# Index columns of a gather copied one group ahead on GpSimd, in a graph network kernel

## The reference

```python
def _L0_gnn_ref(x, edge_index, W1, b1, g1, be1, W2, b2, g2, be2):
    src, dst = edge_index
    edge_features = jnp.concatenate([x[src], x[dst]], axis=1)
    h = edge_features @ W1.T + b1
    h = jax.nn.relu(_batchnorm(h, g1, be1))      # over all edges
    h = h @ W2.T + b2
    edge_updates = jax.nn.relu(_batchnorm(h, g2, be2))
    return jax.ops.segment_sum(edge_updates, dst, num_segments=x.shape[0])
```

## Time and profile before

| | us |
|---|---|
| Median of 3 runs | 4666.78 |
| Lowest and highest run | 4644.99, 4670.69 |
| Profiled execution, whole time | 4677.76 |
| Its span, first to last instruction | 4675.8 |

### The profile page before, as it was taken

The page is one execution under the profiler, slowest core; times in us unless marked ns, Lnnn a source line. Parts: engine busy times, 40 slices in busy tenths (PEclk is TensorE's granted clock), DMA queues, the critical chain, the costliest instruction groups (busy, mean ns, idle before and its releaser), DMA issues. The chain is left out here.

```text
span 4675.8 us, 83038 instructions
## 1 busy us (share of the span) xinstructions
PE 3483.7 (75%) x19041; PEld 1627.4 (35%) x19142; DVE 2879.6 (62%) x3796; ACT 1415.7 (30%) x1952; POOL 1093.9 (23%) x1131
## 2 busy tenths in 40 slices
PE   3776666574889888888877775377789947769994
PEld 2332222252444466665443333122222212222222
DVE  6887767537444455551021113499889949979993
ACT  1123334400222222221011111111088821118880
POOL 3777777666444122120000001000000000000000
PEclk8988878867999899997979997555599955559996
DMA  2345555645999633334838882722033362213331
GB/s 61 115 149 175 185 185 204 211 143 198 350 360 363 234 114 109 101 90 100 251 82 190 187 192 51 133 56 49 21 125 119 112 100 51 54 31 117 125 101 27
DMA packets 808847, 657.35 MB, mean 141 GB/s; under 512 B 599017, under 2 KB 686184, under 8 KB 808516
## 3 DMA queue, kind: packets, MB, share of 16 engines
q1 hardware_dynamic: 677642, 361.12, 29.1%
q10 hardware_dynamic: 106050, 243.93, 15.1%
q0 software_dynamic: 25088, 51.43, 4.3%
HBM read 316.58 MB, written 196.24 MB: 110 GB/s over the span
## 5 line engine op out<-in xcount | busy, mean ns | idle before, releaser
L637 POOL DMA_INDIRECT gat<-a_table,gidx x784 | 908.2, 1158 | 498.9 <-issue 272.7
L1371 DVE CUSTOM_DVE_ANT_0 masked<-psum,mask 128x1564 bf16<-128x1564 f32 x400 | 698.8, 1784 | 176.8 <-ACT mask L937 118.1
L1713 PE MATMUL psum<-qp,kp 96*128 96x391 bf16 x1600 | 589.5, 523 | 285.6 <-DVE mx L1371 160.5
L1406 DVE SCALAR_TENSOR_TENSOR pw<-ex,c_full 128x1564 f32<-128x1564 f32 x400 | 680.8, 1781 | 50.3 <-ACT ex L964 31.5
L1459 PE MATMUL psum<-one_src,one_dst 128*128 x1968 | 471.8, 381 | 271.5 <-issue 153.4
L964 ACT ACTIVATE ex<-psum 128x782 f32<-128x782 f32 x800 | 610.0, 826 | 77.8 <-PE psum L1735 59.8
L1125 DVE TENSOR_SCALAR one_src<-iota_sub,src_low 128x800 f16 x984 | 383.2, 430 | 200.2 <-issue 99.6
L1511 PE MATMUL psum<-c_ring,hp 128*128 128x512 bf16 (+1 forms) x2064 | 422.5, 360 | 75.2 <-DMA c_ring<-c_parts 53.1
L1713 PEld LDWEIGHTS psum<-qp,kp 96*128 x1600 | 173.5, 128 | 701.1 <-issue 701.1
L1459 PEld LDWEIGHTS psum<-one_src,one_dst 128*128 x1968 | 201.0, 106 | 525.9 <-issue 458.2
L1744 PE MATMUL psum<-pw,vaug 128*32 128x391 f32 x3200 | 348.8, 508 | 29.8 <-DVE pw L1406 9.4
(11 more groups left out here) (331 smaller groups left out, 3520.1 us busy)
## 6 DMA issues: line engine op xcount, KB each, us to landing
c_full<-c_whole SPq DMA_DIRECT2D x80, 977.5 KB, 5.0
a_edges<-gat SPq DMA_DIRECT2D x196, 256.0 KB
a_in<-a_edges ACTq DMA_DIRECT2D x98, 512.0 KB
r_edges<-r ACTq DMA_DIRECT2D x98, 512.0 KB
r_in<-r_edges SPq DMA_DIRECT2D x98, 512.0 KB, 3.5
c_whole<-c_sum ACTq DMA_DIRECT2D x100, 400.0 KB
dst_bc<-dst_half ACTq DMA_DIRECT2D x98, 256.0 KB
c_parts<-c_hi ACTq DMA_DIRECT2D x100, 200.0 KB
```

Of the source, the lines that this page charges most:

```text
L637: g.indirect_dma_start(gat[:, s, 2 * k * P:2 * (k + 1) * P], None, a_table, bass.IndirectOffsetOnAxis(ap=gidx[:, s, k:k + 1], axis=0)).the ...
L1371: v.tensor_tensor_reduce(out=masked[:, n % 2, :].rearrange("p (c t) -> p c t", c=4), in0=psum[:, o:o + 4 * BANK].rearrange("p (c t) -> p c ...
L1406: v.scalar_tensor_tensor(pw[:, step_slot(k), :].rearrange("p (h t) -> p h t", h=HQ), ex[:, step_slot(k), :].rearrange("p (h t) -> p h t", ...
L1713: last = t.matmul(bank((n % 2) * 4 + c, CW), kp[0:KQK, n // 2, ds(b * P, P)], qp[0:KQK, n // 2, ((n % 2) * 4 + c) * CW:((n % 2) * 4 + c + ...
```

## The change

There is a new helper `take_rows(i, s)` with the copy alone. In `gather`, the copy of the following group's columns, into the next place of `gidx`, is issued ahead of this group's waits and transfers; the wait on `row_sb` keeps its number, so it now asks for a copy issued one group before. The copy no longer stands behind `gat_free`. The first group's copy stands ahead of everything, and the last round of four stands behind the loop, since its last group has no follower. Number, size and order of the transfers and of the copies stay.

```diff
-            def gather(i):
+            def take_rows(i, s):
+                g.tensor_copy(gidx[:, s, :], src_i[:, ds(16 * i + 4 * s, 4)]).then_inc(S["row_sb"], 1)
+
+            def gather(i, more):
                 for s in range(4):
+                    if s < 3:
+                        take_rows(i, s + 1)
+                    elif more:
+                        take_rows(i + 1, 0)
                     after(pool, gat_free[s], i)
-                    g.tensor_copy(gidx[:, s, :], src_i[:, ds(16 * i + 4 * s, 4)]).then_inc(S["row_sb"], 1)
                     hold("pool", pool, S["row_sb"], 4 * i + s + 1)
...
-                        if k % 2 == 0 and (s or not isinstance(i, int)):
+                        if k % 2 == 0 and (s or not isinstance(i, int) or i):
...
-            gather(0)
-            with pool.Fori(1, NG // 4) as i:
-                gather(i)
+            take_rows(0, 0)
+            gather(0, True)
+            with pool.Fori(1, NG // 4 - 1) as i:
+                gather(i, True)
+            gather(NG // 4 - 1, False)
```

## The result

The changed kernel took 4600.15 us in the median of 5 runs (4595.63 to 4609.23), the kernel before beside it 4666.78 in 5 runs (4644.99 to 4671.9). The ratio is 0.986, 95% interval 0.983 to 0.989. The forecast was 4663, range 4641 to 4678: wrong, 63 us too high. And that is only half of the result. On two other chips, measured later, the same changed kernel is 14.5% and 14.7% **slower** than the kernel before. Both come from the two points that the prediction settled with one sentence each: what the gather does to the other engines, and whether it is off the path.

A forecast was written before the change was run, and what follows sets the result against it. The first pass was taken as held by DMA while the gather runs and by PE afterwards; -4.7 + 0.7 + 0.4 = -3.6 us took the profiled 4677.8 to 4674, 11 us above the median scale, so 4663 us, range 4641 to 4678.

The forecast's parts named there:

- The gather is off the path: First pass: the gather is never late, no stage waits for its end, and it touches the path by its bytes alone.
- Step 1: GpSimd, gap between copy and next transfer: 0.60 us a group saved of 0.88, bounds 0 and 0.86.
- Step 2: Stages ahead of the first pass: 80 us saved on GpSimd, so 12 groups move out of the first pass.
- Step 3: Gather in the first pass: pace stays 8.7 us a group, the gather ends 104 us sooner, near 1439 us.
- Step 4: First pass: 24 units run without the gather, 4.20 us each instead of 4.40, a gain of 4.7 us.
- Its cover: First pass: PE takes whatever DMA gives back beyond 0.20 us a unit.
- Step 5: Stages ahead of the first pass: the denser gather costs 0.7 us by bytes and 0.4 us by slower DVE one-hots.
- Bytes: Rival, first pass: with DMA full, 12 groups' bytes at 362 GB/s give 17 us, time 4651; chance 0.12.
- the gap stays: Rival, GpSimd: the gap stays 0.88 us or DVE's hold-up takes the saving; no group moves, 4667 us; chance 0.20.
- The counting stage pays: Rival, counting stage: denser gather makes ACT's window stores land late, PE waits longer; +45 us, 4712; chance 0.05.
- the second rival: GpSimd: the rival that the gap stays 0.88 us or DVE's hold-up takes all that is saved; chance 0.20.
- no difference: Whole kernel: the change can't be told from none, within about 0.5%, 23 us; chance 0.87, faster 0.07, slower 0.06.

The follow-up runs named there:

- before_again: The kernel before, unchanged, profiled once more on chip 13; 4622.72 us in one execution.
- deep3: The changed kernel with up to three pairs of gather transfers in flight instead of two, on chip 13; 4586.16 us, 0.986 of the kernel before.
- after_fourth: The changed kernel, unaltered, run again on chip 3; 5421.93 us, 1.147 of the kernel before.
- late: The changed kernel with the gather started only behind the counting stage, on chip 0; 5218.21 us.
- beforedeep: The kernel before with up to three pairs of gather transfers in flight instead of two, on chip 6; 4817.67 us, 1.023 of the kernel before.

## Why the prediction was wrong, point by point

**"The gather is off the path", the premise, failed.** It rests on the earlier trace rows, the last gather transfer 37 us ahead of the last load. That was true of that execution. It was not true of the kernel: the earlier trace rows holds because the counting stage was 76 us longer there than in `before_again`, where nothing stalled, and without them the last loads come one by one behind the gather, 13 us apart. The trace had the sign of it. The register rows of L1459 and L1125 are from that profile, and so is PE's wait for "issue", 107.0 us, the largest of its waits in 351 to 927 us. I read the earlier trace rows, which are about data, and never asked why two engines that wait for each other were both idle with nothing to wait for.

**Step 1** was right in kind. The gap fell from 0.88 to 0.16 us, 0.72 us a group, where I took 0.60 and the bounds were 0 and 0.86: an unwaited copy is followed after 0.16 us, another transfer after 0.30. **Step 2** was too small: in the pair without stalls 142 groups had been started when the first pass began, and 162 with the change, 20 more, where I took 12. A group of the counting stage took 6.16 us there instead of 7.09. The gap gives 0.72 of these 0.93 us; and the transfers, which I expected to be held up longer, were shorter, 1146 ns on average instead of 1229. In the profiled pair 160 groups were started (161 copies, 125 + 16 + 20, the last one ahead of its group) against 151, although there were 73 us less.

**Step 3** held for the pace: (1411 - 1091)/35 = 9.1 us a group in the first pass, 8.7 taken. That the gather ended only 28 us below the 1439 I gave is luck: the pass began 73 us earlier than in the forecast, and the gather ended 320 us into it, not 275. **Step 4** held for the execution that I argued from: with the gather 314.0/71 = 4.42 us a unit, behind it 97.0/24 = 4.04 (I said 4.40 and 4.20), and the pass was 6.4 us shorter for my 4.7. Its cover was the failed part: the pass had two limits, DMA and PE, and I left out the third, the gather's own end, since the premise had ruled it out. It is worth 39 us where the stage before is undisturbed.

**Step 5** priced what the denser gather costs the stages ahead at +1.1 us, by bytes and by 17 ns of one-hots a transfer. Without stalls it is near that: the counting stage ends at 851.4 and 854.5 us with the change, 850.6 before, 846.4 without any gather. In the profiled pair the stage went the other way, by -72.6 us, for the kernel before had stalls there and the changed one none; this is the larger part of what was measured, and no step of the prediction had it. Where the changed kernel stalls, the cost is +700 us or more: 1697 and 1723 us on chips 0 and 3, against 947 and 997 for the kernel before on chip 6 (of chips 0 and 3 there is no profile of it; its medians there are within 0.2% of chip 6's, and with three pairs in flight it ends counting at 958 on chip 0).

**The rivals.** "Bytes" and "the gap stays" are out by the unit times and the gap. The 362 GB/s that the bytes rival reckons with are no ceiling either: six stretches of 25 us of `deep3`, from 1100 to 1250 us, moved 364 to 382 GB/s. "The counting stage pays" named the right place, and for chips 0 and 3 the right sign, with a mechanism that plays no part (stores that land late; PE's waits for ACT's copies were 62.5 us in `after_fourth` and 77.8 in the changed kernel on the first chip) and, at 45 us of some 700, a fifteenth of the size. The hold-up of GpSimd by DVE that the second rival rested on fits the runs: in `after_fourth`, where DVE is busy for 271 of 1160 us beside the gather, a transfer takes 1001 ns on average, against 1172 in the counting stage of the changed kernel on the first chip (DVE busy for 637 of 774 us) and 1244 in that of the kernel before (642 of 846 us). That DVE is what holds it is read from these numbers; no run changes DVE's work alone. The cost of the gather for PE and DVE comes by their sequencers, whose register instructions took up to 1426 and 1415 ns there.

**The chances.** I gave 0.87 to "no difference" on one profile of one chip. The measured ratio, 0.983 to 0.989, is clear of 1. I took the spread of three runs, 26 us, for noise around one shape of the execution. The spread could have told that something differs between executions by more than the change was forecast to bring, and that one profile can't show what.

## What to carry to other kernels

A claim that a transfer chain is off the path is a claim on the stages ahead of it: before it is used, say how long each of them would be if nothing disturbed it, and ask whether the chain is still early then. Where two engines are idle together "for issue" and the longest of their register instructions takes many medians, as here (1340 ns against 51 on PE, 1374 against 93 on DVE, with a counting stage of 927 us that took 851 without stalls), a change near it must be priced with and without that. And a GpSimd loop of indirect transfers made denser should be measured on several chips: taking out a wait of under 1 us in each group, which reads as pure loss, went with a loss of 15% on two of the chips here and a gain of 1.3 to 1.4% on two others.

## What the runs showed of the hardware

While GpSimd issued indirect transfers, many register and branch instructions of PE and DVE, and of SP, GpSimd and ACT too, took some 0.70 to 0.73 us each (the median stall of each trace is 0.700 to 0.708) instead of 0.03 to 0.1, in four of the six comparisons (the first, and chips 6, 0 and 3). The 1561 stalls of `after_fourth` are 703 of PE, 516 of DVE, 257 of SP, 71 of GpSimd and 14 of ACT, and 909 of them end within 0.05 us of a stall of another engine; in `late` it is 4 of 146. In the kernel before with three pairs in flight the stalls reached into the first pass. `beforedeep`, 1238 to 1395 us:

```profile
1238.00:1395.00 157.00, 86.32 (x344) 38.55 (x351) 23.86 (x54) 15.64 (x13) 106.29 (x133) 0.67 0.62 208
```

ACT takes 13 instructions in 157 us there, with 18 stalls; behind the gather's end it takes 40 in 160 us (1440 to 1600). The trace's two instruction queues (q8 and q14) move 7 packets between 80 and 1240 us of `after_fourth`, beside 1561 stalls, and 15 in the same stretch of the changed kernel on the first chip, beside none; so a stall is not a wait for a packet of its own there. No run here shows what the instructions wait for.

TensorE's granted clock stands at 1.00 or 0.50 of full speed in the trace of `after_fourth`. Its mean there is 0.55 over the 1160 us with the gather, in which PE is busy for 317 us, so mostly the lower of the two, and 0.90 over the 483 us behind it, in which PE is busy for 331.
